# A recurrent mixer and a routed expert layer: finished expert rows scattered from each pair into the output

## The chip, the cores and the metric
The kernel runs on one core of a Trainium2 chip. The metric is the device time of one execution in microseconds; the median of three runs of the kernel before is 650.63 us (649.58 to 650.96).

## What is computed
Input x is (4, 1024, 128), float32. A first layer normalises x, makes queries, keys, values, gates and decays, and runs a recurrence over time with an 8x8 state for each of 16 heads. Its output is laid out so that only every third token gets a non-zero value:

```python
z = jnp.zeros_like(o)
out3 = jnp.stack([z, z, o], axis=2).reshape(B, 3 * N, H, HD)
out = out3[:, -N:]
```

So only a third of the tokens (342 of 1024 in each sequence, the *mixed* rows) is changed by the first layer; the *other* rows keep their x. The second layer adds to every row a shared network and one of 16 experts:

```python
logits = x @ w_router.T
_, top_idx = jax.lax.top_k(logits, TOP_K)            # TOP_K = 1
scores = jax.nn.sigmoid(logits) * mask
masked_inputs = scores.T[:, :, None] * x[None, :, :]
gate_up = jnp.einsum('eth,ehf->etf', masked_inputs, gate_up_proj)
expert_out = jnp.einsum('etf,efh->eth', up * jax.nn.silu(gate), down_proj)
out = shared + expert_out.sum(axis=0)                # then x + out
```

## The kernel before
**Rows.** `xf` holds the residual, 33 rows of 128 numbers in each of the 128 partitions. Every third one is a mixed row (11, set `MIXED`), the rest are other rows (22, set `OTHERS`). Some of the slots stand for no token.

**The recurrence.** The time axis is cut into chunks, 32 for each sequence. First the matrices and sums of all chunks grow side by side (up to about 308 us). Then `ch_s`, the state at the start of each chunk, is found by a chain of 63 steps on VectorE (DVE), L1569 and L1574: `ch_m` (8x8 matrix of a chunk) times the state gives products `ch_pr`, laid out as [value, output i, input j], with the chunk's own sum as a ninth j that GpSimd (POOL) copies in at L1138; the reduction over j is the next state:

```python
V.tensor_tensor(ch_pr[:, m % 2, :, :, 0:HD], ch_m[r][:, :, i, :]..., ch_s[:, :, i, :]..., ALU.mult)
V.tensor_reduce(ch_s[:, :, i + 1, :].rearrange("p i v -> p v i"), ch_pr[:, m % 2], AX.X, ALU.add)
```

A second recursion of 11 steps (L1461 to L1482, L1982) runs behind it from the states found.

**Experts.** For each set of rows the router's choice gives every row a slot in a list that is sorted by expert and cut into tiles of 128 slots (38 tiles for the other rows, 26 for the mixed ones). Rows times score are scattered by POOL into DRAM (`xs_...`, `scatter_tile`, L1021, one indirect DMA for each of the set's row slots). Tiles are worked on in pairs, `over_pairs`: SP loads the rows of a pair (L515), PE transposes them (`x_transposes`, L1919), multiplies by the two experts' first matrices (`gate_up`, L1925), ScalarE (ACT) takes silu (L900), DVE multiplies (`gate`, L1360), PE transposes (L1932) and multiplies by the second matrices (`down`, L1942) into one PSUM region `b_y`; ACT copies it to `e_y` (`copy_y`, L909), which frees `b_y` for the next pair's `down`, and SP writes it to DRAM (`ys_...`, L522). `RUNS[0]`, 12 pairs of other rows, stands beside the chain, `RUNS[1]`, 7 pairs, beside the second recursion, and `RUNS[2]`, the 13 pairs of the mixed rows, at the end. `over_pairs` writes the last three or four pairs out and puts those before into a loop of two pairs a turn. PE, ACT and DVE work one pair ahead and the loads up to three.

**Shared network.** `shared` works in groups of four row slots (L1855 to L1865 on PE, L859 on ACT, L1346 and L1351 on DVE). `shared_add` adds the result to `xf` and counts `s_fa`. For the other rows it runs beside the first part of the chain, for the mixed ones right ahead of `RUNS[2]`.

**The end.** When the pairs of the other rows are written, POOL gathers them back in row order into SBUF (`gather`, L1037, 22 indirect DMAs from 512.7 us on). DVE adds them to `xf` at L1636, in one instruction of 2,816 elements a partition, ahead of the pairs of `RUNS[2]`. After the thirteenth pair is written, POOL gathers the mixed rows (11 indirect DMAs), DVE adds them in two parts (L1647), and SP and ACT store the sums. SP's stores of the other rows (20, L672 to L676) are in its queue behind the last pair's.

Order is by hand: each engine has its own list, and semaphores count what is ready (`s_et` transposed pairs, `s_eo` finished `e_y`, `s_ey` finished `down`, `s_ew` pairs written, `s_gat` gathered, `s_fin` final rows).

Of the kernel before, what the change touches and what calls it, by code (L numbers as in the profile page):

```python
# [65 lines left out]

def constants():
# [13 lines left out]
    for t in (OTHERS, MIXED):  # L81
        v = valid[:, t.rows]
        parts["valid_" + t.name] = v
        spare = np.where(v, 0, t.tiles * P + np.cumsum(~v.ravel()).reshape(v.shape) - 1)
        parts["spare_" + t.name] = spare
        assert (~v).sum() <= P
    parts["prefer"] = np.tile(E - np.arange(E)[None, :], (P, 1))
# [104 lines left out]
def build(nc, a, out, xs, ys, scr):  # L192

    ctx = ExitStack()
    with ctx:
# [7 lines left out]
        normed = nc.dram_tensor("normed", (B, N, D), F32).ap()  # L203

# [4 lines left out]
        eps = sb("eps", [P, 1])  # L209
        warm = sb("warm", [P, 4])  # L210
# [20 lines left out]
        ch_pr = early[:, at:at + 2 * 4 * HD * (HD + 1)].rearrange("p (b v i j) -> p b v i j", b=2, v=4, i=HD)  # L231
# [87 lines left out]
        for t in (MIXED, OTHERS):  # L319
# [12 lines left out]
            else:  # L332
                rows, scaled = take(t.n * D), take(t.n * D)
                q["rows"] = q["shared"] = [rows[:, j * D:(j + 1) * D] for j in range(t.n)]
                q["scaled"] = [scaled[:, j * D:(j + 1) * D] for j in range(t.n)]
                q["back"] = rows
# [23 lines left out]
        def xT_shared(t, g):  # L360
# [9 lines left out]
        assert 4 * U * P <= left.shape[1]  # L370
        e_in, e_xT = (left[:, k * 2 * U * P:(k + 1) * 2 * U * P].rearrange("p (b u d) -> p b u d", b=2, u=U)
                      for k in (0, 1))
# [40 lines left out]
        s_gat, s_fin, s_out = {t: two("s_gathered_" + t) for t in fb}, sem("s_final"), sem("s_out")  # L413
        s_ends = sem("s_out_ends")
# [3 lines left out]
        PARTS = ((0, MIXED.n // 2 + 1), (MIXED.n // 2 + 1, MIXED.n))  # L418
# [55 lines left out]
        def over_pairs(engine, run, pair):  # L474
# [3 lines left out]
            looped = (n - 3) // 2 * 2  # L478
            with engine.Fori(0, looped // 2) as half:
                i = half * 2  # L480
                for k in (0, 1):
                    pair(i, k, 3)
# [17 lines left out]

        def middle_rows(b):

            n = 3 * SKIP
            return out[b, ROWS - n:(C - 1) * ROWS - n:3, :].rearrange("(g r) d -> g r d", r=L2)
# [25 lines left out]
        def _(sp):  # L530
# [72 lines left out]
            for t in SETS:  # L603
                sp.dma_start(xs[t.name].rearrange("(m p) d -> p m d", p=P),
                             zeros[:, 0:D].unsqueeze(1).to_broadcast([P, t.tiles + 1, D])).then_inc(s_xz, 16)
                sp.dma_start(ys[t.name][t.tiles * P:, :], zeros[:, 0:D]).then_inc(s_xz, 16)
# [59 lines left out]
            pairs_in_out(sp, RUNS[2])  # L666
            n = 3 * SKIP
            last = N - ((C - 1) * ROWS - n)
            sp.wait_ge(s_fin, 1)
            for b in range(B):  # L670
                g0 = b * C
                sp.dma_start(out[b:b + 1, 1:ROWS - n, :], xf[g0:g0 + 1, n + 1:, :]).then_inc(s_out, 16)  # L672
                for q in (1, 2):
                    sp.dma_start(out[b, ROWS - n + q:(C - 1) * ROWS - n:3, :].rearrange("(g r) d -> g r d", r=L2),
                                 xf[g0 + 1:g0 + C - 1, q::3, :]).then_inc(s_out, 16)
                    sp.dma_start(out[b:b + 1, N - last + q:N:3, :],  # L676
                                 xf[g0 + C - 1:g0 + C, q:last:3, :]).then_inc(s_out, 16)
            for part, (lo, hi) in enumerate(PARTS):
                sp.wait_ge(s_fin, 2 + part)
                for b in range(B):  # L680
                    sp.dma_start(middle_rows(b)[:, lo:hi, :], xf[b * C + 1:b * C + C - 1, 3 * lo:3 * hi - 2:3, :]
                                 ).then_inc(s_out, 16)
            sp.wait_ge(s_out, 16 * 7 * B)
            sp.wait_ge(s_ends, 16 * 2 * B)
# [1405 lines left out]
```

## Time and profile before

| | |
|---|---|
| median of the runs | 650.63 us (649.58 to 650.96, 3 runs) |
| the profiled execution | 648.87 us, span of its instructions 647.1 us |
| mean granted TensorE clock | 0.946 of 2.4 GHz |
| busy, share of the span | PE 80%, DVE 76%, POOL 56%, ACT 40% |
| chain that ended last, by engine | PE 35%, DVE 29%, issue 14%, POOL 12%, DMA 4%, ACT 3% |
| DMA | 41.79 MB in 46,946 packets |

The time of an execution is a little longer than its span. The span begins with the first instruction and ends with the last; a time in the time line is counted from its start. PEld is the load of a matrix into PE, which overlaps the products. Busy shares are averages over stages with different limits, so the time line of a stage says more than they do.

### The profile page before, as it was taken

The page shows a single profiled execution, that of the slowest core. Times are in us where ns is not written, and L with a number is a line of the kernel's source. Part 1 is how long each engine was busy: PE and PEld are TensorE (multiplying, and loading weights), DVE is VectorE, ACT ScalarE, POOL GpSimd, SP SyncE. Part 2 cuts the span into 40 slices and gives each one's busy share as a digit, 9 for nine tenths or more (in the row PEclk, how much of TensorE's full clock was granted, in tenths as well). Part 3 has the DMA queues.
Part 4 walks back from the last instruction along what each step waited for, and adds up shares of the span by engine and source line. Part 5 has one row for each costly group of instructions (what it writes and reads, how often), then busy time and mean ns, then how long its engine had stood idle before and what let it go on. Part 6 is the DMA issues. An engine that isn't in the chain of part 4 may idle for free.

```text
span 647.1 us, 7400 instructions
## 1 busy us (share of the span) xinstructions
PE 516.5 (80%) x1809; PEld 269.2 (42%) x1810; DVE 489.2 (76%) x787; ACT 257.0 (40%) x542; POOL 363.1 (56%) x353
## 2 busy tenths in 40 slices
PE   3889899999999885777776889789999956398830
PEld 2543434444444332322444455434443353355520
DVE  5697999989898998999799997788999656322201
ACT  4477543444444432112442345524554115044510
POOL 2378776757576564764786343567766574600033
PEclk9999999999999999988999899989999968889985
DMA  7701138400000691000711133101100011112134
GB/s 179 191 18 32 33 89 217 113 1 1 1 1 1 171 344 38 1 0 0 187 43 41 42 97 73 50 9 32 32 16 9 13 54 32 53 50 65 57 85 114
DMA packets 46946, 41.79 MB, mean 65 GB/s; under 512 B 4700, under 2 KB 40360, under 8 KB 46536
## 3 DMA queue, kind: packets, MB, share of 16 engines
q1 hardware_dynamic: 43332, 35.61, 20.2%
q0 software_dynamic: 2448, 5.38, 3.0%
q10 hardware_dynamic: 1136, 0.46, 0.3%
q8 instruction: 12, 0.20, 0.1%
q14 instruction: 18, 0.15, 0.1%
HBM read 23.80 MB, written 17.63 MB: 64 GB/s over the span
## 4 chain that ended last, share of the span: by engine, by line
PE 35%; DVE 29%; issue 14%; POOL 12%; DMA 4%; ACT 3%; SPq 0%; POOLq 0%; DVEq 0%; ACTq 0%
PE ps L1925 10%; DVE grown L1468 9%; PE ps L1942 5%; POOL grown L1091 4%; DVE ps L1502 4%; PE ps L1878 3%; PE ps L1932 2%; DVE early L1569 2%; DVE grown L1490 2%; PE ps L1982 2%; PE ps L1683 2%; POOL uv L1008 2%; PE ps L1879 2%; POOL early L1037 2%; PE ps L1983 2%
## 5 line engine op out<-in xcount | busy, mean ns | idle before, releaser
L1091 POOL TENSOR_TENSOR grown<-grown 128x512 f32<-128x512 f32 x64 | 80.5, 1267 | 91.6 <-DVE grown L1490 91.6
L1468 DVE TENSOR_TENSOR grown<-ps,steps 128x1536 f32<-128x1536 f32 x64 | 112.1, 1752 | 1.6
L1878 PE MATMUL ps<-grown,cst 128*128 128x512 f32 x128 | 72.7, 650 | 25.3 <-DVE grown L1468 24.7
L883 ACT ACTIVATE uv<-ps 128x512 f32<-128x512 f32 x64 | 38.1, 597 | 104.8 <-DVE grown L1490 104.8
L1925 PE MATMUL ps<-steps 128*128 x128 | 68.8, 635 | 8.4 <-issue 8.2
L1008 POOL TENSOR_TENSOR uv<-uv,steps 128x512 f32<-128x512 f32 x64 | 67.4, 1075 | 1.9 <-ACT uv L883 1.9
L1879 PE MATMUL ps<-grown,cst 128*128 128x512 f32 x128 | 67.1, 606 | 0.0
L1360 DVE TENSOR_TENSOR e_h<-rk,ps 128x256 f32<-128x256 f32 x64 | 25.4, 418 | 53.4 <-ACT rk L900 34.6
L1888 PE MATMUL ps<-uv,cst 128*128 128x512 f32 x128 | 60.4, 594 | 0.6 <-POOL uv L1008 0.6
L1167 POOL TENSOR_TENSOR early<-state,qT 128x512 f32 x22 | 37.1, 1688 | 34.0 <-DVE state L1482 34.0
L1490 DVE TENSOR_TENSOR grown<-ps,steps 128x512 f32<-128x512 f32 x64 | 43.3, 676 | 7.4 <-PE ps L1878 7.4
L1502 DVE TENSOR_TENSOR ps<-ps,grown 128x512 f32<-128x512 f32 x60 | 41.6, 693 | 9.4 <-POOL grown L1091 9.4
L1037 POOL DMA_INDIRECT early<-ys_mixed,slots_mixed x11 | 10.5, 956 | 64.7 <-DMA ys_mixed<-e_y 61.7
L1496 DVE TENSOR_TENSOR ps<-ps,steps 128x512 f32<-128x512 f32 x64 | 44.1, 689 | 1.1 <-PE ps L1879 1.0
L1878 PEld LDWEIGHTS ps<-grown,cst 128*128 128x128 f32 x128 | 21.0, 196 | 57.2 <-DVE grown L1468 51.2
L1138 POOL COPY early<-early 128x32 f32<-128x32 f32 x63 | 27.2, 434 | 28.1 <-DVE early L1574 28.0
L1569 DVE TENSOR_TENSOR early<-early 128x256 f32<-128x256 f32 x63 | 40.1, 636 | 1.3
L900 ACT ACTIVATE rk<-ps 128x256 f32<-128x256 f32 x64 | 23.9, 383 | 39.9 <-PE ps L1925 38.2
L1879 PEld LDWEIGHTS ps<-grown,cst 128*128 128x128 f32 x128 | 25.2, 197 | 32.2 <-issue 32.2
L1942 PE MATMUL ps<-steps,e_hT 128*128 x256 | 35.9, 284 | 2.8 <-ACT e_hT L904 2.7
L1888 PEld LDWEIGHTS ps<-uv,cst 128*128 128x128 f32 x128 | 24.2, 190 | 31.8 <-issue 29.6
L1942 PEld LDWEIGHTS ps<-steps,e_hT 128*128 128x128 f32 x256 | 31.5, 191 | 9.1 <-issue 8.0
(228 smaller groups left out, 1008.0 us busy)
## 6 DMA issues: line engine op xcount, KB each, us to landing
steps<-gate_up_proj SPq DMA_DIRECT2D x1, 4096.0 KB, 16.7
xs_others<-zeros SPq DMA_DIRECT2D x1, 2496.0 KB, 11.0
steps<-xs_others SPq DMA_DIRECT2D x19, 128.0 KB, 2.2
ys_others<-e_y SPq DMA_DIRECT2D x19, 128.0 KB, 1.8
early<-chain_m SPq DMA_DIRECT2D x4, 512.0 KB, 6.3
xf<-x SPq DMA_DIRECT2D x4, 495.0 KB
normed<-early SPq DMA_DIRECT2D x28, 64.0 KB, 1.7
xs_mixed<-zeros SPq DMA_DIRECT2D x1, 1728.0 KB, 8.9
```

The lines of the kernel that those rows point to most:

```text
L1008: return G.tensor_tensor(wide(dst, w), wide(src, w), per_col(tile, k, 1, h, w), ALU.mult)
L1091: G.tensor_tensor(decayed[:, h], decayed[:, h], work[:, h, 1], ALU.add).then_inc(s_add[h], 1)
L1468: V.tensor_tensor(grown[:, :, h].rearrange("p e (x w) -> p e x w", w=HD), st, per_col(tile, FF, 3, h, HD), ALU.mult).then_inc(s_prod[h], 1)
L1490: V.tensor_tensor(wide(work[:, h, 1], HD), wide(ps[h][:, 1], HD), per_col(tile_of(i), PP, 1, h, HD), ALU.mult).then_inc(s_uterm[h], 1)
L1496: V.tensor_tensor(wide(bank[2 * h], HD), wide(bank[2 * h], HD), per_col(tile_of(i), K, 1, h, HD), ALU.mult).then_inc(s_term[h], 1)
L1502: V.tensor_tensor(dst, bank[2 * h], decayed[:, h], ALU.add).then_inc(s_state[h], 1)
L1569: V.tensor_tensor(ch_pr[:, m % 2, :, :, 0:HD], ch_m[r][:, :, i, :].rearrange("p j i -> p i j").unsqueeze(1) .to_broadcast([P, 4, HD, HD]), ...
L1878: T.matmul(bank[2 * h + 1], c["block"], work[:, h, 1], start=True, stop=True).then_inc(s_usum[h], 1)
L1879: T.matmul(bank[2 * h], c["minus"], work[:, h, 0], start=True, stop=True).then_inc(s_red[h], 1)
L1888: T.matmul(bank[4 + h], c["ident"], vterm[:, h], start=i in (0, L1), stop=i + 1 in (L1, NT)).then_inc(s_ba[h], 1)
L1925: T.matmul(b_gu(run, b)[u], e_xT[:, b, u], gu[:, bass.ds(ex * (2 * F), 2 * F)], start=True, stop=True).then_inc(s_eg, 1)
L1942: ins = T.matmul(b_y(run)[:, u * D:(u + 1) * D], e_hT[:, u, f * P:(f + 1) * P], dw[:, bass.ds(ex[u] * F + f * D, D)], start=(f == 0), stop ...
```

## The change
Four things are changed.

1. **Mixed rows go straight from the pair into the output.** Each scattered mixed row carries a 129th number, its token's row in the output (`token_mixed`, `q["sent"]`, DRAM tensor `slot_rows`); slots without a row hold 4096, one past the last row. SP loads rows of 129 numbers (`load_rows`). POOL turns the pair's two columns of row numbers into integers (`tokens`). `add_base` on DVE takes the place of ACT's `copy_y`: PSUM plus the pair's *base* rows gives `e_y`. Then two indirect DMAs for each pair write `e_y` to the output rows; numbers above 4095 are dropped by a bounds test.
2. **Base rows.** The residual with the shared network's part (`xf`, mixed rows) is scattered by slot into `ys_mixed` ahead of the pairs, 11 indirect DMAs, with the row numbers of pairs 0 and 1 taken between them; `load_base` brings a pair's 256 rows back. `ys_mixed` is zeroed as a whole at the start, and `slot_rows` filled with rows of zeros and 4096.
3. **Other rows.** Their add is cut in two (12 and 10 row slots) and stands behind `add_base` of pairs 0 and 1. SP stores them two DMAs a pair between its loads, after waiting for both halves (`s_fin` 2). The gathers, adds and stores of the mixed rows at the end are gone, and pairs 0 and 1 of this run are written out ahead of the loop.
4. **The chain.** `ch_pr` is laid out as [value, input j, output i], so that the product reads and writes runs of eight; the reduction steps over eight elements.

```diff
-        ch_pr = early[:, ...].rearrange("p (b v i j) -> p b v i j", b=2, v=4, i=HD)
+        ch_pr = early[:, ...].rearrange("p (b v j i) -> p b v j i", b=2, v=4, i=HD)
...
+            alone = 2 if run.t is MIXED else 0
+            looped = alone + (n - 3 - alone) // 2 * 2
+            for k in range(alone):
+                pair(0, k, n - 1 - k)
...
+            def load_rows(k):
+                sp.wait_ge(s_et, k + run.g0 - 1 if k >= 2 else run.g0)
+                if k >= 2:
+                    sp.wait_ge(s_to, k - 1)
+                sp.dma_start(e_row[:, k % 2], x_in[:, k * U:(k + 1) * U, :]).then_inc(s_ei[k % 2], 16)
+
+            def load_base(k):
+                sp.wait_ge(s_eo, k + run.g0)
+                sp.dma_start(e_base[:, k % 2], base_in[:, k * U:(k + 1) * U, :]).then_inc(s_eb[k % 2], 16)
...
+            for k in range(3):
+                load_rows(k)
+            sp.wait_ge(s_based, 16 * MIXED.n)
+            for k in range(2):
+                load_base(k)
+            for k in range(2, run.n):
+                if k + 1 < run.n:
+                    load_rows(k + 1)
+                load_base(k)
+                if k == 2:
+                    sp.wait_ge(s_fin, 2)
+                for b, part in stores[2 * k - 4:2 * k - 2]:
+                    store_others(b, part)
...
-            pool.wait_ge(s_fa, GA[MIXED.name] + len(MIXED.groups))
-            m = RUNS[2].n
-            gather(MIXED, (RUNS[2].base[0] + (m + 1) // 2, RUNS[2].base[1] + m // 2))
+            for g, (lo, hi) in enumerate(MIXED.groups):
+                pool.wait_ge(s_fa, GA[MIXED.name] + g + 1)
+                for j in range(lo, hi):
+                    G.indirect_dma_start(ys[MIXED.name], ... q["idx"][:, j:j + 1] ..., xf[:, MIXED.rows[j]], None
+                                         ).then_inc(s_based, 16)
+                    if j in TOKENS_AT:
+                        tokens(TOKENS_AT.index(j))
+            for k in range(run.n):
+                if k + 2 < run.n:
+                    tokens(k + 2)
+                pool.wait_ge(s_to, k + 1)
+                pool.wait_ge(s_eo, k + run.g0 + 2)
+                for u in range(U):
+                    G.indirect_dma_start(out_rows, ... e_to[:, k, u:u + 1] ..., e_y[:, k % 2, u], None,
+                                         bounds_check=B * N - 1, oob_is_err=False).then_inc(s_sent[k % 2], 16)
...
-            V.tensor_tensor(rows_of(xf, OTHERS, 0, OTHERS.n), rows_of(xf, OTHERS, 0, OTHERS.n),
-                            tiles_of(fb[OTHERS.name]["back"], OTHERS), ALU.add).then_inc(s_fin, 1)
...
+                add_base(i, k)
+                if ahead > 3 and k < 2:
+                    lo, hi = ((0, 12), (12, OTHERS.n))[k]
+                    dve.wait_ge(s_gat, 16 * OTHERS.n)
+                    V.tensor_tensor(rows_of(xf, OTHERS, lo, hi), ..., ALU.add).then_inc(s_fin, 1)
```

`add_base` waits for the pair's `down`, its base rows and the scatter of `e_y` two pairs before.

POOL, behind the gathers of the other rows: L1021 scatters mixed rows and L1037 gathers before; the list before ends so.

```order
L1037 DMA early<-ys_others,slots_others 128x128 x21
L1021 DMA xs_mixed<-early,slots_mixed 3456x128 [waits s_scaled,s_slots,s_slots_zeroed]
L1021 DMA xs_mixed<-early,slots_mixed 3456x128 [waits s_scaled] x10
L1037 DMA early<-ys_mixed,slots_mixed 128x128 [waits s_e_written1,s_e_written0,s_f_added]
L1037 DMA early<-ys_mixed,slots_mixed 128x128 x10
L195 UNCONDITIONAL_BRANCH
```

The same place in the changed kernel, up to the second pair's scatters (L1060 scatters rows, L1225 base rows, L1220 is `tokens`, L1237 writes to the output):

```order
L1060 DMA slot_rows<-early,slots_mixed 3456x129 [waits s_scaled] x10
L1225 DMA ys_mixed<-xf,slots_mixed 3456x128 [waits s_f_added]
L1225 DMA ys_mixed<-xf,slots_mixed 3456x128 x3
L1225 DMA ys_mixed<-xf,slots_mixed 3456x128 [waits s_f_added]
L1220 CAST e_to<-steps 128x2 [waits s_e_transposed]
L1225 DMA ys_mixed<-xf,slots_mixed 3456x128 x3
L1225 DMA ys_mixed<-xf,slots_mixed 3456x128 [waits s_f_added]
L1220 CAST e_to<-steps 128x2 [waits s_e_transposed]
L1225 DMA ys_mixed<-xf,slots_mixed 3456x128 x2
L1220 CAST e_to<-steps 128x2 [waits s_e_transposed]
L1237 DMA out<-e_y,e_to 4096x128 [waits s_e_out,s_e_tokens]
L1237 DMA out<-e_y,e_to 4096x128
```

The gathers behind the last pair are gone; eleven scatters stand ahead of the first pair's output, and two scatters and a copy follow for each pair.

SP, where the mixed pairs begin in the changed kernel (L691 is `load_rows`, L695 `load_base`, L703 and L705 are stores of the other rows):

```order
L691 DMA steps<-slot_rows 128x2x129 [waits s_e_transposed,s_scattered_mixed]
L691 DMA steps<-slot_rows 128x2x129 [waits s_e_transposed]
L691 DMA steps<-slot_rows 128x2x129 [waits s_e_tokens,s_e_transposed]
L695 DMA uv<-ys_mixed 128x2x128 [waits s_e_out,s_bases_scattered]
L695 DMA uv<-ys_mixed 128x2x128 [waits s_e_out]
L691 DMA steps<-slot_rows 128x2x129 [waits s_e_tokens,s_e_transposed]
L695 DMA uv<-ys_mixed 128x2x128 [waits s_e_out]
L703 DMA out<-xf 1x256 [waits s_final]
L705 DMA out<-xf 330x1x128
L691 DMA steps<-slot_rows 128x2x129 [waits s_e_tokens,s_e_transposed]
```

Before, this was a load ahead of each pair and a store behind it; now the fourth load of rows stands behind the wait for the base rows, and the fifth behind the wait for both halves of the other rows' add and two stores.

DVE, the start of the mixed pairs in the changed kernel (L1423 is `gate`, L1709 `add_base`, L1719 the other rows' add):

```order
L1423 TENSOR_TENSOR e_h<-rk,ps 128x256 [waits s_e_silu]
L1709 TENSOR_TENSOR e_y<-ps,uv 128x256 [waits s_e_written0,s_e_base0,s_e_y]
L1719 TENSOR_TENSOR xf<-xf,early 128x6x256 [waits s_gathered]
L1423 TENSOR_TENSOR e_h<-rk,ps 128x256 [waits s_e_silu,s_e_h_transposed]
L1423 TENSOR_TENSOR e_h<-rk,ps 128x256 [waits s_e_silu]
L1709 TENSOR_TENSOR e_y<-ps,uv 128x256 [waits s_e_written1,s_e_base1,s_e_y]
L1719 TENSOR_TENSOR xf<-xf,early 128x5x256 [waits s_gathered]
```

Before, the list had one add of 128x11x256 ahead of the first `gate`, and nothing but `gate` in the pairs.

## Rows read from the trace of the kernel before

**Rows 1.** Time line, 620 to 638 us: start us, us, engine, line, operation, names, [idle before]
```profile
620.89 0.38 ACT L909 ACTIVATE e_y<-ps 128x256 f32<-128x256 f32 x1 [1.45 <-PE ps L1942]
621.72 0.32 SPq L672 DMA_DIRECT2D out<-xf  x1
622.09 1.02 SPq L674 DMA_DIRECT2D out<-xf  x1
...
623.91 0.99 POOL L1037 DMA_INDIRECT early<-ys_mixed,slots_mixed  x1 [61.66 <-DMA ys_mixed<-e_y]
...
636.52 0.95 POOL L1037 DMA_INDIRECT early<-ys_mixed,slots_mixed  x1 [0.30 <-issue]
```
**Rows 2.** Time line, 557 to 567 us
```profile
557.83 0.97 POOL L1021 DMA_INDIRECT xs_mixed<-early,slots_mixed  x1 [0.30 <-issue]
...
558.32 3.08 DVE L1636 TENSOR_TENSOR xf<-xf,early 128x2816 f32<-128x2816 f32 x1
559.10 3.15 POOL L1021 DMA_INDIRECT xs_mixed<-early,slots_mixed  x1 [0.30 <-issue]
...
565.96 0.66 PE L1919 MATMUL ps<-cst,steps 128*128 128x128 f32 x2 [8.15 <-DMA steps<-xs_mixed]
```
**Rows 3.** Time line, copies of the first three mixed pairs' results
```profile
574.26 0.38 ACT L909 ACTIVATE e_y<-ps 128x256 f32<-128x256 f32 x1 [0.52 <-PE ps L1942]
...
578.05 0.38 ACT L909 ACTIVATE e_y<-ps 128x256 f32<-128x256 f32 x1 [0.61 <-PE ps L1942]
...
582.46 0.38 ACT L909 ACTIVATE e_y<-ps 128x256 f32<-128x256 f32 x1 [0.53 <-PE ps L1942]
```
**Rows 4.** Busy time by stretch: length, PE, PEld, DVE, ACT, POOL busy (x), PEclk, DMA, GB/s
```profile
566.00:572.00 6.00, 5.53 (x15) 2.72 (x16) 0.84 (x2) 1.83 (x5) 0.00 (x0) 0.66 0.15 44
...
580.00:590.00 10.00, 9.06 (x49) 5.91 (x48) 2.27 (x6) 5.53 (x14) 0.00 (x0) 1.00 0.23 66
```
**Rows 5.** Groups by line and shape: count | busy us, mean ns | idle before
```profile
L1569 DVE TENSOR_TENSOR early<-early 128x256 f32<-128x256 f32 x63 | 40.1, 636 | 1.3
L1574 DVE TENSOR_REDUCE early<-early 128x32 f32<-128x288 f32 x63 | 28.6, 455 | 5.1 <-POOL early L1138 3.2
L1360 DVE TENSOR_TENSOR e_h<-rk,ps 128x256 f32<-128x256 f32 x64 | 25.4, 418 | 53.4 <-ACT rk L900 34.6 <-PE ps L1932 18.7
L1138 POOL COPY early<-early 128x32 f32<-128x32 f32 x63 | 27.2, 434 | 28.1 <-DVE early L1574 28.0
...
L1271 DVE TENSOR_TENSOR early<-early 128x352 f32<-128x352 f32 x1 | 0.9, 880 | 0.0
L1326 DVE TENSOR_TENSOR early<-ps,early 128x176 f32<-128x176 f32 x1 | 0.5, 465 | 0.0
L1328 DVE TENSOR_TENSOR early<-early 128x176 f32<-128x176 f32 x1 | 0.3, 342 | 0.0
```
**Rows 6.** Time line: two adds of the shared network, and the second recursion's start
```profile
334.40 0.69 DVE L1351 TENSOR_TENSOR xf<-xf,ps 128x512 f32<-128x512 f32 x1
...
341.65 0.69 DVE L1351 TENSOR_TENSOR xf<-xf,ps 128x512 f32<-128x512 f32 x1
...
401.72 0.90 POOL L1127 DMA_DIRECT2D state<-chain_s  x1 [2.27 <-DMA chain_s<-early]
...
408.17 0.38 ACT L909 ACTIVATE e_y<-ps 128x256 f32<-128x256 f32 x1 [1.45 <-PE ps L1942]
```
**Rows 7.** DMA issues: queue, count, KB each, median us from issue to landing
```profile
steps<-xs_mixed SPq DMA_DIRECT2D x13, 128.0 KB, 2.1
ys_mixed<-e_y SPq DMA_DIRECT2D x13, 128.0 KB, 1.8
...
early<-chain_b SPq DMA_DIRECT2D x4, 256.0 KB, 3.7
...
xs_mixed<-early,slots_mixed POOLq DMA_INDIRECT x11, 2.2
```
**Rows 8.** The page's DMA line: busy tenths in 40 slices
```profile
DMA  7701138400000691000711133101100011112134
```

More of the change, by code:

```diff
@@ L332, in build @@
             else:
-                rows, scaled = take(t.n * D), take(t.n * D)
+                rows, scaled = take(t.n * D), take(t.n * (D + 1))
                 q["rows"] = q["shared"] = [rows[:, j * D:(j + 1) * D] for j in range(t.n)]
-                q["scaled"] = [scaled[:, j * D:(j + 1) * D] for j in range(t.n)]
-                q["back"] = rows
+                q["sent"] = [scaled[:, j * (D + 1):(j + 1) * (D + 1)] for j in range(t.n)]
+                q["scaled"] = [r[:, 0:D] for r in q["sent"]]
+                q["token"] = scaled.rearrange("p (n d) -> p n d", d=D + 1)[:, :, D]
                 q["lg"] = take(t.n * E)
@@ L667, in _, with store_others @@
+            def load_base(k):
+                sp.wait_ge(s_eo, k + run.g0)
+                sp.dma_start(e_base[:, k % 2], base_in[:, k * U:(k + 1) * U, :]).then_inc(s_eb[k % 2], 16)
             n = 3 * SKIP
             last = N - ((C - 1) * ROWS - n)
-            sp.wait_ge(s_fin, 1)
-            for b in range(B):
+            def store_others(b, part):
                 g0 = b * C
[L672 to L684, printed above, removed]
+                if part == 0:
+                    sp.dma_start(out[b:b + 1, 1:ROWS - n, :], xf[g0:g0 + 1, n + 1:, :]).then_inc(s_out, 16)
+                elif part < 3:
+                    sp.dma_start(out[b, ROWS - n + part:(C - 1) * ROWS - n:3, :].rearrange("(g r) d -> g r d", r=L2),
+                                 xf[g0 + 1:g0 + C - 1, part::3, :]).then_inc(s_out, 16)
+                else:
+                    sp.dma_start(out[b:b + 1, N - last + part - 2:N:3, :],
+                                 xf[g0 + C - 1:g0 + C, part - 2:last:3, :]).then_inc(s_out, 16)
@@ new lines, in _ @@
+            stores = [(b, part) for b in range(B) for part in range(5)]
+            for k in range(3):
[11 more added lines that the diff above has]
+                    store_others(b, part)
@@ L685, in _ @@
+            sp.wait_ge(s_out, 16 * 5 * B)
+            for k in (0, 1):
+                sp.wait_ge(s_sent[k], 16 * U * ((run.n + 1 - k) // 2))
         @block.scalar
@@ L996, in _ @@
             pairs(RUNS[2])
-            n = 3 * SKIP
-            last = N - ((C - 1) * ROWS - n)
-            act.wait_ge(s_fin, 3)
-            for b in range(B):
-                g0 = b * C
-                act.dma_start(out[b:b + 1, 0:1, :], xf[g0:g0 + 1, n:n + 1, :]).then_inc(s_ends, 16)
-                act.dma_start(out[b:b + 1, N - last:N:3, :], xf[g0 + C - 1:g0 + C, 0:last:3, :]).then_inc(s_ends, 16)
         def pool_tt(dst, src, tile, k, h, w):
```

102 lines of the change are left out of this document (69 added, 33 removed).

## The prediction
> **What bounds the kernel now.** I read the end first, in the time line: it shows what is left after the last matrix work. The last pair's result is copied out of PSUM at 620.89 to 621.27. POOL then waits until it has landed in DRAM and issues eleven gathers, from 623.91 to 637.47; DVE's add and the stores of the sums follow, and the span ends at 647.1 [rows 1]. So 25.8 us (647.1 - 621.27) hold no matmul: a round trip of the results through DRAM. That is the part the change can remove.
>
> Next the start of the last run of pairs. Indirect transfers follow each other every 1.27 us (557.83, 559.10). The last one took 3.15 us instead of 0.97: it stood beside DVE's 3.08 us add of the other rows, which began at 558.32. Only when it had landed could the first pair be loaded, and its first transposes ran at 565.96 [rows 2]. In the pairs the reader is to look at the ends of the PSUM copies: 574.64, 578.43, 582.84, and 621.27 for the thirteenth. That is 38.4 us for the ten pairs after the third, and 4.4 or 3.8 us each in turn; PE fills them at the full clock (9.1 of 10 us busy) [rows 1, 3, 4].
>
> Last the chain of states, 308 to 398 us. A step is a product of 0.64 us and a reduction of 0.46 us on DVE [rows 5]. Beside it run six groups of the other rows' shared network, 7.25 us apart (334.40, 341.65), then twelve pairs. The recursion behind waits for the last of these pairs' copies, 408.17 + 0.38, while the chain's last result was sent on at 401.72 [rows 6].
>
> **The change part by part**, against the profiled execution (span 647.1, time 648.87; that is 1.76 below the median of the runs, 650.63, so I carry the difference over to the median).
>
> *The end.* Gone: the wait for the written pair, 11 gathers, two adds, the stores of the mixed rows. New behind the last pair: DVE's add (0.42 us, by the 128x256 products from PSUM [rows 5]; it stands for the copy of 0.38) and two scatters. POOL started 0.8 us after what it waited for (landing 1.8 us after the issue at 621.3, so 623.1, to 623.91 [rows 1, 7]); the second issue comes 1.27 later and lands 2.2 us after it began [rows 2, 7]: 4.3 us in place of 25.8. **Minus 21.5.**
>
> *Base rows.* POOL gets 11 more scatters, ahead of the pairs' own. DVE's long add no longer stands beside the last row scatter, so this begins at 559.10 and takes 0.97. The eleventh base scatter begins 11 x 1.27 later, plus two small POOL copies for the row numbers (0.43 us each by the 128x32 copy [rows 5], part of it in the usual gap: 0.6 for both): 559.1 + 14.0 + 0.6 = 573.7; it lands at 575.9. SP loads the first two bases (0.4 us an issue, 2.1 to land): at 578.0 the first is there, and the first add ends at 578.4, not 574.6. **Plus 3.8.** Queued behind this wait on SP is the load of pair 3's rows: 576.7 + 2.1 = 578.8. PE needs them ahead of pair 1's last products, so these run 579.2 to 580.4.
>
> *The other rows' add.* It was 3.08 us in an idle stretch; now 12 and 10 row halves, about 1.75 and 1.48 us by the same rate (0.15 us + 1.04 ns an element), behind the first and second base add. The first holds gate 2, and add 1 ends at 581.4 (was 578.43: plus 3.0). The second ends at 582.9. SP waits for it (s_fin), issues two stores (0.32 and 1.02 [rows 1]), and only then loads pair 4's rows: 584.4 + 2.1 = 586.5. PE stands before their transposes; transposes, products and add take 0.4 + 1.1 + 0.5 + gaps, so add 2 ends at 588.7, not 582.84: **plus 5.9** in all, which contains the 3.8. From pair 3 on SP is ahead again: stores of at most 1.9 us a pair, and a load is issued a pair and a half before PE needs it.
>
> *The clock.* In the 6 us behind PE's long idle stretch the granted clock was 0.66 on average, a mixture of the lower level (1.2 GHz) and the higher (2.4), and from 580 to 590 it was 1.00 [rows 4]. PE now idles about 5 us twice: before pair 1's last products and before pair 2's. The missing 0.34 of 6 us is 2 us of lost work; for the two together I set none to 2.5 us on the path, **plus 1.2**.
>
> *Loop.* Two pairs stand alone ahead of it, so one turn less: the difference of 4.4 and 3.8, **minus 0.5**.
>
> *POOL in the pairs.* Per pair two scatters and a copy: 2 x 1.27 + 0.4 = 2.9 us of 3.9; hidden by PE's work. The bounds test on the row numbers is in no row; I take 0.97 us a scatter as the nearest, with ends 0.97 and 3.15 (the held one). ScalarE loses its copy, off the path. DVE's loop gets a third instruction and register waits; it is idle over half of it.
>
> *Zeroing and 516-byte rows.* SP zeroes 3.5 MB instead of 1.8 for this set. That falls in slices 7 and 8 of 40 (16.2 us each), and behind them stand five slices with no DMA time [rows 8]: hidden. Rows of 129 numbers in place of 128 may load slower; zero to 1.6 us each (the next size, 256 KB, landed in 3.7 [rows 7]), twice on the path. I take zero.
>
> *The chain.* The product now reads and writes runs of eight; the reduction steps over eight elements (32 bytes). Rows: a 128x256 product read in runs takes 0.42, the chain's 0.64. A 128x176 add takes 0.34 with runs and 0.47 with one SBUF operand at a step of 44 bytes (L1328, L1326), 0.70 ns an element; a 128x352 add with a step of 88 bytes 0.88 (L1271), where 0.15 us and 1.04 ns an element make 0.52, so 1.0 ns an element [rows 5]. So the product gains 0.21 us; if the reduction pays the same for its 288 elements it loses 0.20 to 0.29. The sum is 0 to +0.08 a step, 63 steps: 0 to +5. If a single stream pays nothing, a step gains 0.21 us, a group at most 0.35 (then PE and ScalarE lead), six groups 2; the pairs behind do not gain, since they are PE's with or without a chain (4.0 us each in both runs). I take **0**: L1326 is a single SBUF stream too, its other operand being PSUM. The Trainium skill (SBUF — State Buffer, "Door 1: The DMA port swizzle") speaks against this edit in the same way: SBUF is read in lines of 16 bytes, and a step onto a new line each time costs, beyond 4 fp32 elements. By that rule alone the reduction would pay and the sum stay at 0; the trace agrees with it on two-operand instructions, and shows no reduction with a step.
>
> *Sum:* -21.5 + 5.9 + 1.2 - 0.5 + 0 = **-14.9**; 647.1 becomes 632.2, and the median 650.6 becomes **635.7**.
>
> **Rivals.**
> 1. *The reduction's step is free* (25%). For: a reduction reads one stream only. Against: L1326. Another 2 us: 633.7.
> 2. *516-byte rows load slowly* (14%). No row has them. Twice 1.6 on the path, perhaps a little in the loop: 639.
> 3. *POOL takes the pairs over, in part* (7%). At 1.9 us a scatter (double) a pair needs 2 x 2.2 + 0.4 = 4.8 us, 0.9 over PE's 3.9, twelve times: 646.
> 4. *POOL is held* (4%): a scatter to tested row numbers costs as much as the one that was held, 3.15. A pair takes 2 x 3.45 + 0.4 = 7.3, the last add comes at 578.4 + 88 = 666, the end at 673, time 676: slower. It decides from about 2.2 us a scatter: 578.4 + 12 x 5.4 + 4.3 + 1.2 reaches about 648. For it: POOL can be held by DVE, as the row shows. The Trainium skill (SBUF — State Buffer, "SBUF: two separate sides") calls this a lock on a shared port, taken among others by a DVE instruction with two SBUF inputs. By that rule only the two long adds would hold scatters here, for 3.2 us in all, in time that POOL has spare. Against the rival: in the loop DVE reads one PSUM operand each time, and beside such instructions scatters took 0.97 [rows 2].
> 5. *That the change doesn't do what it says*: the gathers are gone from the order of POOL; nothing for it.
>
> **Numbers.** Forecast 50%, rivals 25, 14, 7, 4. Around the forecast the unknown terms are -1.7 (clock 0 and a little) to +2.5 (chain, clock). The range leaves out rival 4, most of 3 and the far end of 1: 631 to 641. A measurement tells 0.2%, 1.3 us, from no change; all cases but the fourth are far above it. Faster 0.95, same 0.01, slower 0.04.
>
> **What would show it.** Right: no row of gathers from ys_mixed; two scatters of about 0.97 us per pair; about 5 us from the last products to the end; adds 0, 1, 2 ending near 578.4, 581.4, 588.7; PE waiting for a load of slot rows before pair 2's transposes; product near 0.42 and reduction near 0.66 us; the recursion's first products near 408.6. Wrong: scatters above 1.5 us, pairs above 4 us with POOL as releaser, or pairs that start before 575.

## The result, and the profile after

The changed kernel takes 642.15 us (median of 4 runs, 641.85 to 642.69) where the kernel before takes 650.41 beside it: a ratio of 0.9875, interval 0.9858 to 0.9892. It is faster, as forecast, but by 8.3 us and not by 14.9; the range of 631 to 641 does not hold it. The profiled execution took 641.85 us, with a span of 639.7 in place of 647.1. The forecast for the span was 632.2.

One thing has to be known to compare single profiles (*before* is that of the kernel before, *after* that of the changed kernel, the others carry the names of the experiments). In the stretch from 512 to 546 us, ahead of the mixed pairs, PE's granted clock was 0.75 of 2.4 GHz in the profiles of before, a1, a3, a4, b1, b3, b4, c1 and c2, and 0.70 in those of after, a2, b2, c3 and c4, a mixture of its two levels (1.2 and 2.4 GHz) each time. With 0.70 the way from the first gather of the other rows to the shared network's first add for the mixed rows is 1.8 us longer (35.93 us in after, 34.14 in a1). From 240 to 300 us the clock also differs, and the chain starts anywhere from 306.7 to 310.2 us. So the first transposes of the mixed pairs stand at 560.6 to 565.7 us in kernels that are the same up to there, and runs of one kernel lie up to 6 us apart (c1: 645.56 to 651.94). So I take distances inside a profile, and medians.

The end in the changed kernel, in the time line (start us, us, engine, line, operation, names, idle before), which answers to [rows 1]:

```profile
627.15 0.42 DVE L1709 TENSOR_TENSOR e_y<-ps,uv 128x256 f32<-128x256 f32 x1 [0.35 <-PE ps L2016]
628.43 0.98 POOL L1237 DMA_INDIRECT out<-e_y,e_to  x1 [1.50 <-DVE e_y L1709]
629.63 0.42 DVE L1709 TENSOR_TENSOR e_y<-ps,uv 128x256 f32<-128x256 f32 x1 [2.06 <-PE ps L2016]
629.71 0.98 POOL L1237 DMA_INDIRECT out<-e_y,e_to  x1 [0.30 <-issue]
631.00 0.98 POOL L1237 DMA_INDIRECT out<-e_y,e_to  x1 [0.30 <-issue]
632.29 0.98 POOL L1237 DMA_INDIRECT out<-e_y,e_to  x1 [0.30 <-issue]
```

The gathers are gone. The last add ends at 630.05 and the last scatter is issued until 633.27. Nothing is busy after that, and yet the span ends at 639.7, which is 9.65 us after the last add. What fills this time is in the view of the block's own line, L202 (queue, instruction, count: shortest, median and longest ns, first and last start):

```profile
L202 POOLq DRAIN  x1: 8258/8258/8258, 631.2 to 631.2; - x1
L202 SPq COMPARE_BRANCH  x1: 38/38/38, 634.5 to 634.5; - x1
L202 SPq DRAIN  x1: 13/13/13, 634.7 to 634.7; - x1
L202 SPq EVENT_SEMAPHORE  x1: 17/17/17, 639.6 to 639.6; - x1
```

SP has seen all transfers land at 634.5. POOL's queue drains from 631.2 to 639.5, which is 6.2 us beyond the end of its last scatter, and the last instructions of the other engines' queues start at 639.6 to 639.7, behind it. The same line in the kernel before, where it was number L195:

```profile
L195 POOLq DRAIN  x1: 14907/14907/14907, 628.4 to 628.4; - x1
L195 SPq COMPARE_BRANCH  x1: 38/38/38, 646.7 to 646.7; - x1
L195 SPq DRAIN  x1: 13/13/13, 646.9 to 646.9; - x1
```

There the drain ended at 628.4 + 14.9 = 643.3, and POOL's last gather had been issued until 637.47: it reached 5.8 us beyond the last gather, nearly as far as in the changed kernel, and was hidden behind the stores.

The start of the mixed pairs, which answers to [rows 2, 3]:

```profile
559.61 0.97 POOL L1060 DMA_INDIRECT slot_rows<-early,slots_mixed  x1 [0.30 <-issue]
...
564.32 0.66 PE L1993 MATMUL ps<-cst,steps 128*128 128x128 f32 x2 [5.96 <-DMA steps<-slot_rows]
...
573.71 0.97 POOL L1225 DMA_INDIRECT ys_mixed<-xf,slots_mixed  x1 [0.31 <-issue]
...
575.97 0.87 SPq L695 DMA_DIRECT2D uv<-ys_mixed  x2
576.93 0.42 SPq L691 DMA_DIRECT2D steps<-slot_rows  x1
578.18 0.42 DVE L1709 TENSOR_TENSOR e_y<-ps,uv 128x256 f32<-128x256 f32 x1 [6.19 <-DMA uv<-ys_mixed]
578.52 1.75 DVE L1719 TENSOR_TENSOR xf<-xf,early 128x1536 f32<-128x1536 f32 x1
...
579.50 1.65 POOL L1237 DMA_INDIRECT out<-e_y,e_to  x1 [4.62 <-DVE e_y L1709]
579.86 1.91 PE L2016 MATMUL ps<-steps,e_hT 128*128 x8
...
581.81 0.42 DVE L1709 TENSOR_TENSOR e_y<-ps,uv 128x256 f32<-128x256 f32 x1 [0.88 <-PE ps L2016]
582.15 1.48 DVE L1719 TENSOR_TENSOR xf<-xf,early 128x1280 f32<-128x1280 f32 x1
...
585.10 0.51 SPq L691 DMA_DIRECT2D steps<-slot_rows  x1
...
587.74 0.44 PE L1993 MATMUL ps<-cst,steps 128*128 128x128 f32 x2 [2.09 <-DMA steps<-slot_rows]
...
589.98 0.42 DVE L1709 TENSOR_TENSOR e_y<-ps,uv 128x256 f32<-128x256 f32 x1 [3.38 <-PE ps L2016]
```

This came as drawn: the last row scatter is no longer held, the last base scatter begins at 573.71, DVE waits 6.19 us for base rows, PE waits twice for a load of slot rows, and adds 0, 1 and 2 end at 578.60, 582.23 and 590.40 (forecast 578.4, 581.4, 588.7, with 1.2 us more for the clock).

The chain, by the groups by line and shape (count | busy us, mean ns of one), against [rows 5]:

```profile
L1637 DVE TENSOR_REDUCE early<-early 128x32 f32<-128x288 f32 x63 | 42.6, 676 | 4.3 <-POOL early L1178 2.2
L1632 DVE TENSOR_TENSOR early<-early 128x256 f32<-128x256 f32 x63 | 27.3, 433 | 1.3
L1178 POOL COPY early<-early 128x32 f32<-128x32 f32 x63 | 19.3, 307 | 34.4 <-DVE early L1637 34.2
```

The product fell from 636 to 433 ns, the reduction rose from 455 to 676: together 18 ns more a step. The chain as a whole kept its length, as its first reduction shows, here in before and in after:

```profile
309.86 0.46 DVE L1574 TENSOR_REDUCE early<-early 128x32 f32<-128x288 f32 x1 [0.21 <-POOL early L1138]
308.93 0.68 DVE L1637 TENSOR_REDUCE early<-early 128x32 f32<-128x288 f32 x1 [0.17 <-POOL early L1178]
```

From there until its last result is sent on it took 91.9 us before (to 401.72) and 91.6 after (to 400.48).

### The profile page after: what moved, and what is told of

Same layout as the page of the kernel before. It is cut to its first block, busy times and chain, and to the rows that moved or that the text cites. A ratio compares the mean times of both kernels' runs of the same rounds, so it can differ in the third digit from the quotient of the medians.

```text
span 639.7 us, 7393 instructions
## 1 busy us (share of the span) xinstructions
PE 522.9 (82%) x1809; PEld 273.2 (43%) x1810; DVE 493.5 (77%) x799; ACT 252.4 (39%) x530; POOL 382.3 (60%) x394
## 4 chain that ended last, share of the span: by engine, by line
PE 34%; DVE 31%; issue 16%; POOL 13%; ACT 3%; DMA 2%; SPq 1%; POOLq 0%; DVEq 0%; ACTq 0%
DVE grown L1531 10%; PE ps L1999 8%; PE ps L2016 5%; POOL grown L1131 5%; DVE ps L1565 4%; PE ps L1952 3%; DVE early L1637 3%; PE ps L2006 2%; PE ps L2056 2%; POOL uv L1045 2%; DVE early L1632 2%; DVE grown L1553 2%; PE ps L1757 2%; POOL slot_rows L1060 2%; PE ps L2057 2%
## 5 line engine op out<-in xcount | busy, mean ns | idle before, releaser
L1131 POOL TENSOR_TENSOR grown<-grown 128x512 f32<-128x512 f32 x64 | 80.5, 1268 | 91.7 <-DVE grown L1553 91.7
L1999 PE MATMUL ps<-steps 128*128 x128 | 70.1, 646 | 8.2 <-issue 8.2
L1423 DVE TENSOR_TENSOR e_h<-rk,ps 128x256 f32<-128x256 f32 x64 | 25.2, 417 | 42.7 <-ACT rk L943 29.4
L1637 DVE TENSOR_REDUCE early<-early 128x32 f32<-128x288 f32 x63 | 42.6, 676 | 4.3 <-POOL early L1178 2.2
L1237 POOL DMA_INDIRECT out<-e_y,e_to x26 | 26.2, 1008 | 27.0 <-DVE e_y L1709 22.6
L1178 POOL COPY early<-early 128x32 f32<-128x32 f32 x63 | 19.3, 307 | 34.4 <-DVE early L1637 34.2
L2016 PE MATMUL ps<-steps,e_hT 128*128 x256 | 37.2, 290 | 2.7 <-ACT e_hT L947 2.7
```

The source lines that it names most:

```text
L1131: G.tensor_tensor(decayed[:, h], decayed[:, h], work[:, h, 1], ALU.add).then_inc(s_add[h], 1)
L1999: T.matmul(b_gu(run, b)[u], e_xT[:, b, u], gu[:, bass.ds(ex * (2 * F), 2 * F)], start=True, stop=True).then_inc(s_eg, 1)
L2016: ins = T.matmul(b_y(run)[:, u * D:(u + 1) * D], e_hT[:, u, f * P:(f + 1) * P], dw[:, bass.ds(ex[u] * F + f * D, D)], start=(f == 0), stop ...
```

## The experiments

Two questions: what the 5.3 us are that the end took beyond the forecast (theories A to D in the texts below), and which of the terms at the pairs' start hold. Edits are against the changed kernel where nothing else is said.

**a1: POOL waits for its scatters to land.**

```diff
+            for k in (0, 1):
+                pool.wait_ge(s_sent[k], 16 * U * ((run.n + 1 - k) // 2))
```

> The changed kernel (time 642.15, span 639.7; last scatters issued 631.00 and 632.29, landed about 634.6), and POOL itself waits for both counts of landed scatters before its list ends. Theory A: POOL's drain ends a fixed 6 us after its last indirect DMA was issued, whatever POOL does meanwhile: span 639.7 unchanged, time 642 +- 1. Theory B: the drain is some 6 us of work that begins only when POOL's list has ended: POOL then ends at about 634.8 + 6 = 641, time 643.5 or more. Theory C: the drain only waits for the landed bytes, so behind a wait for them it is over at once: span about 635.5, time 638.

641.82 us (639.28 to 643.32), ratio 0.9881 [0.9857, 0.9905]. The median tells nothing: it lies at theory A's value, and two of the four runs took 643.2 and 643.3 us, as theory B has it, the two others 639.3 and 640.4. The drain's rows do:

```profile
L202 POOLq COMPARE_BRANCH  x1: 38/38/38, 630.9 to 630.9; - x1
L202 POOLq DRAIN  x1: 6197/6197/6197, 631.1 to 631.1; - x1
```

With everything landed at 630.9 the drain still took 6.2 us. The end came 7.8 us behind the last scatter's issue (628.74 + 0.98 = 629.72, to 637.5), where after has 6.4 (633.27 to 639.7). So the drain is not a wait for bytes: it takes 6.2 us that begin when POOL's list has ended. Theory B.

**a2: no scatters for the last pair.**

```diff
-            for k in range(run.n):
+            for k in range(run.n - 1):
```

> The changed kernel without the two scatters of the thirteenth pair (the output lacks these 256 slots' rows); SP waits for the last add instead. POOL's last indirect DMA is then that of the twelfth pair, issued about 627.6 + 1.3 + 1 = 629.9 at the end, the last add ends at 630.05. Theory A (a fixed 6.2 us behind the last indirect DMA): span about 636.1, time 638.5. Theory C (the end follows the landing of the last bytes, about 2.4 us behind the issue): span about 632.5, time 635. If the drain is tied to neither but to the end of the other engines' lists, it stays near 639.

639.85 us (639.18 to 639.99), 0.984 [0.9823, 0.9856]: 2.3 us less. POOL's last issue ended at 631.74 and the span at 638.0, 6.3 later; SP was done at 633.2. The end moves with POOL's list, not with the landing. (Counted with the router of the reference and its inputs, the mixed rows fill 17 of the 26 tiles. So the last four pairs hold no token's row and their scatters write nothing; with these inputs a2 leaves nothing out of the output, unlike what the text above says. POOL's issues for them take 0.98 us all the same.)

**a3: the rows' loads first.**

```diff
-            for k in range(3):
+            for k in range(4):
                 load_rows(k)
             sp.wait_ge(s_based, 16 * MIXED.n)
...
-                if k + 1 < run.n:
+                if 3 < k + 1 < run.n:
                     load_rows(k + 1)
                 load_base(k)
-                if k == 2:
+                if k == 3:
                     sp.wait_ge(s_fin, 2)
-                for b, part in stores[2 * k - 4:2 * k - 2]:
+                for b, part in stores[2 * k - 6:2 * k - 4] if k > 2 else []:
```

> The changed kernel with two loads moved in SP's list: pair 3's rows ahead of the wait for the base rows, pair 4's rows ahead of the wait for the other rows' add, whose stores begin a pair later. Theory 1 (the two waits of PE for a load of slot rows, 4.4 and 2.1 us, set pairs 1 and 2): add 1 is then held by the base rows and DVE's long adds only, add 2 ends about 4 us earlier (586.4 instead of 590.4), and the time is 638 (637 to 639.5). Theory 2 (the base rows and the long adds on DVE set them, loads only fill the gap): add 2 ends less than 1.5 us earlier, time 640.7 to 642.

636.91 us, 0.9802 [0.9788, 0.9816]: 5.2 us less. From the first transposes to the end of add 2 it takes 21.9 us (560.89 to 582.80) where after has 26.1 (564.32 to 590.40): 4.2 us, theory 1.

```profile
574.56 0.42 DVE L1709 TENSOR_TENSOR e_y<-ps,uv 128x256 f32<-128x256 f32 x1 [4.88 <-DMA uv<-ys_mixed]
...
577.23 0.42 DVE L1709 TENSOR_TENSOR e_y<-ps,uv 128x256 f32<-128x256 f32 x1
...
582.38 0.42 DVE L1709 TENSOR_TENSOR e_y<-ps,uv 128x256 f32<-128x256 f32 x1 [0.40 <-PE ps L2016]
```

Add 2 follows add 1 in 5.2 us instead of 8.2: that is pair 4's load, which stood behind the wait for DVE's second long add and two stores. Add 1 follows add 0 in 2.7 instead of 3.6, but it does so in b1 too (2.66), where no load was moved and pair 1's last products took 1.23 us and not 1.91. So moving pair 3's load is not shown to have gained anything at add 1; against b1 3.1 of 3.8 us are pair 2's (8.3 to 5.2), the rest lies ahead of add 0.

**a4 and c1: the chain alone.** a4 undoes part 4 of the change in the changed kernel; c1 makes it in the kernel before:

```diff
-        ch_pr = early[:, ...].rearrange("p (b v i j) -> p b v i j", b=2, v=4, i=HD)
+        ch_pr = early[:, ...].rearrange("p (b v j i) -> p b v j i", b=2, v=4, i=HD)
```

> The changed kernel with the chain's product laid out as before (product 636 ns, reduction 455 ns, POOL's copy 434 ns in place of 433, 676 and 307). By the sum of the groups (-18 ns a step for the old one, 63 steps) the old layout would be 1.1 us faster if the chain were the bound; the time line showed the opposite, the new one 1.3 us ahead at the start of the second recursion, through POOL's shorter copy, and given back behind it. Theory 1 (a step's price is the same in both): 642.1 +- 1, no difference to be told. Theory 2 (the shorter copy counts, and what was lost behind has another cause): 643.4. Theory 3 (only DVE's sum counts): 641.0.

> The kernel before with part 4 of the change alone (chain's product in runs, reduction with a step). Theory 1 (a step of the chain has the same price, 1.11 us of DVE against 1.09): 650.3 +- 1, no difference. Theory 2 (POOL's shorter copy, 307 ns for 434, counts): 1.2 us less, 649.1. Theory 3 (the reduction's 18 ns count): 1.1 us more.

a4: 640.8 us (638.41 to 642.79), 0.986 [0.9834, 0.9885], which overlaps that of after. c1: 649.28 us, 0.9995 [0.9976, 1.0014]. The groups follow the layout in both (product and reduction 638 and 455 ns in a4, 436 and 677 in c1). a4 leans to theory 3 and c1 to theory 2, opposite ways and within the spread. The profiles settle more than the times: from the first reduction to the last result sent on it takes 91.7 to 91.9 us with the old layout (before, b3, b4, a4) and 91.5 to 92.1 with the new one. The chain's new layout is worth nothing that can be measured, either way.

**b1, b2, b3: the block's end without POOL's drain.**

```diff
-        block = ctx.enter_context(nc.Block())
+        block = ctx.enter_context(nc.Block(no_gpsimd_drain=True))
```

b1 is the changed kernel with this line, b2 adds the edit of a3, b3 is the kernel before with it. SP's waits for the last landings stay.

> The changed kernel, its instructions the same; only the block's end is built without the drain of POOL's queue (SP still waits until every transfer has landed). Theory B (6.2 us of POOL's own drain, which starts when POOL's list ends, set the end): the end follows SP's wait for the last landing, about 2.4 us behind the last issue, instead of 7.2 us: span 4 to 5 us shorter, time 637.5 (636.5 to 638.5). Theory D (some 6 us belong to the end of any such program, whichever engine they are booked on): 642 +- 1.

> The same block end together with the loads moved ahead in SP's list (the kernel of a3_rows_first, 636.9). Theory B: the two gains add, 636.9 - 4.6 = 632.3 (631 to 633.5). Theory D: 636.9 +- 1.

> The kernel before, its block's end built without POOL's drain. There the drain ended at 643.3, the landing of the last stores at about 646.7: it was hidden, with 3.4 us to spare. Theory B: 650.4 +- 1, no difference. Theory D: no difference either.

b1: 636.1 us, 0.9788 [0.9762, 0.9815], 6.0 us less than after. In its profile no DRAIN stands on POOL's queue, and the end is SP's:

```profile
L202 SPq COMPARE_BRANCH  x1: 37/37/37, 630.5 to 630.5; - x1
L202 SPq DRAIN  x1: 13/13/13, 630.7 to 630.7; - x1
```

The last add ends at 626.05 and the span at 631.0: 4.95 us, where after has 9.65. So the drain's own part is 4.7 us; the rest of the 6.0 is not explained by it (b1's profile has the clock of 0.75 in 512 to 546, and after's has 0.70). b2: 632.25 us, 0.9718 [0.9686, 0.9749]: the two gains add. b3: 649.23 us, 0.9987 [0.9971, 1.0004]: in the kernel before the drain cost nothing.

**b4: the kernel before without its last adds and stores** (SP waits for the gathers instead; the mixed rows are missing from the output).

> The kernel before without the last adds and stores of the mixed rows (the output lacks these rows' expert part and the rows themselves); SP waits for the gathers' landing, which were issued until 637.5 and land at about 639.5. Theory B: with DVE, ACT and SP out of the way POOL's drain sets the end, 637.5 + 5.8 = 643.3 and 0.2: span 643.5, time 646.2 by the median, 4 us less than before. Rival C (the end follows the landing): span 640, time 642.5.

645.84 us, 0.9919 [0.9893, 0.9945]: 4.5 us less, not the 8 that the landing would give.

```profile
L195 POOLq DRAIN  x1: 14905/14905/14905, 628.1 to 628.1; - x1
L195 SPq DRAIN  x1: 13/13/13, 639.6 to 639.6; - x1
```

SP had finished at 639.6; the drain ended at 643.0, the span at 643.3. The hidden wait of the kernel before comes out as soon as its cover is gone, which is what the change did.

**c2: the other rows' adds back ahead of the pairs.**

```diff
+            for lo, hi in ((0, 12), (12, OTHERS.n)):
+                dve.wait_ge(s_gat, 16 * OTHERS.n)
+                V.tensor_tensor(rows_of(xf, OTHERS, lo, hi), ..., ALU.add).then_inc(s_fin, 1)
             gate(RUNS[2], 0, 0, 0)
...
                 add_base(i, k)
-                if ahead > 3 and k < 2:
...
```

> The changed kernel with the other rows' two adds moved back ahead of the pairs (behind the shared network's last add, about 559 to 562), the loads as in the change. Theory 1 (the add behind the base adds, and SP's wait for it, put 2 to 3 us on pairs 1 and 2; ahead of the pairs it holds one base scatter for about 2 us): add 2 ends some 2 us earlier, time 640 (639 to 641). Theory 2 (what the held scatter costs and what the pairs gain are equal): 642. Theory 3 (a scatter held ahead of the pairs costs more than the pairs gain): 643 or more.

637.3 us, 0.9822 [0.98, 0.9844]: 4.9 us less, more than theory 1 said. By distance, first transposes to the end of add 2: 22.8 us (561.43 to 584.21) against 26.1, 3.3 us less. Add 1 ends 3.6 us after add 0, as in after; add 2 follows in 4.8 instead of 8.2. So all of it is at pair 2, whose load no longer waits behind DVE's add in the pairs. What the adds hold ahead of the pairs is small:

```profile
555.96 1.83 POOL L1060 DMA_INDIRECT slot_rows<-early,slots_mixed  x1 [0.30 <-issue]
558.10 1.10 POOL L1225 DMA_INDIRECT ys_mixed<-xf,slots_mixed  x1 [0.30 <-issue]
```

That is 0.86 + 0.13 us. The first of them stands ahead of the first transposes; counted from the start of the shared network's last add, which takes it in, it is 29.5 us (554.73 to 584.21) against 32.0 (558.39 to 590.40), 2.5 us less. Moving the add into the pairs was worth nothing as SP's list stood: it saved 1 us of held scatters and put some 3.3 on pair 2. The rest of the 4.9 us between the medians is not explained.

**c3: no base scatters** (the loads stay and read zeros; the output lacks the residual and the shared network's part of the mixed rows).

> The changed kernel without the eleven scatters of the base rows and the wait for them; the loads of base rows stay and read the zeroed tensor (the output lacks the residual and the shared network's part of the mixed rows). It prices the base rows' way, for which the prediction took 3.8 us at pair 0 (5.9 with the other rows' add at pair 2). Theory 1 (base scatters set pair 0, and through the load behind them pair 1 and 2): add 0 ends at about 573, the end comes 5.5 to 6.5 us earlier: 636. Theory 2 (the long adds and the load behind s_fin set pair 2 anyway): 2 us or less earlier: 640.

635.04 us, 0.9781 [0.9761, 0.9802]: 7.1 us less. The last row scatter stands at 559.61 as in after, so here times compare directly:

```profile
572.29 0.42 DVE L1702 TENSOR_TENSOR e_y<-ps,uv 128x256 f32<-128x256 f32 x1 [0.34 <-PE ps L2009]
...
584.50 0.42 DVE L1702 TENSOR_TENSOR e_y<-ps,uv 128x256 f32<-128x256 f32 x1 [4.56 <-PE ps L2009]
```

Add 0 ends 5.9 us earlier, add 2 5.5, the last add 6.0 (624.01). Theory 1: the way of the base rows is dear at pair 0 and never given back. Add 2 still comes 8.5 us after add 1, so the load behind the wait for DVE's long add is a price of its own, paid with or without base scatters. (The medians are 7.1 us apart, 1 more than the last adds; that is not explained.)

**c4: row, token number and base row in one scatter.** The kernel of b2, with rows of 257 numbers: DVE's add of the shared network writes into the tile that POOL scatters, each scatter waits for its group's add, and base rows are loaded from the same DRAM tensor.

```diff
-                V.tensor_tensor(rows_of(xf, t, lo, hi), rows_of(xf, t, lo, hi), ...
+                V.tensor_tensor(fb[t.name]["base"][:, lo:hi, :] if t is MIXED else rows_of(xf, t, lo, hi),
+                                rows_of(xf, t, lo, hi), ...
...
                 for j in range(lo, hi):
-                    G.indirect_dma_start(ys[MIXED.name], ..., xf[:, MIXED.rows[j]], None).then_inc(s_based, 16)
+                    scatter_tile(MIXED, j)
```

> A new version: the kernel of b2_no_drain_rows_first (632.25), in which DVE writes xf plus the shared network's result next to the scaled row and its token number, and POOL scatters the three together, 257 numbers, after the shared network's group: 11 scatters in place of 22. The last one is then tied to the last group's add: it starts about 2 us later than the last row scatter did, and 12 us earlier than the last base scatter did. Theory 1 (with the base rows in time, pairs 0 to 2 follow from the first transposes as before, 16.9 us up to the third result): add 2 ends 2 to 3 us earlier, 629.8 (628.5 to 631.5). Theory 2 (the long adds on DVE set pairs 1 and 2, or rows of 1,028 bytes scatter slowly): 632 or more.

630.31 us (629.44 to 631.95), 0.9713 [0.9693, 0.9733]; b2 had 632.25.

```profile
561.32 0.97 POOL L1059 DMA_INDIRECT slot_rows<-early,slots_mixed  x1 [0.31 <-issue]
...
566.32 0.66 PE L1992 MATMUL ps<-cst,steps 128*128 128x128 f32 x2 [8.41 <-DMA steps<-slot_rows]
...
574.81 0.42 DVE L1708 TENSOR_TENSOR e_y<-ps,uv 128x256 f32<-128x256 f32 x1 [0.34 <-PE ps L2015]
...
583.01 0.42 DVE L1708 TENSOR_TENSOR e_y<-ps,uv 128x256 f32<-128x256 f32 x1 [0.47 <-PE ps L2015]
```

The last scatter begins at 561.32 in place of 573.71, and a scatter of twice the bytes takes the same 0.97 us. First transposes to add 2: 17.1 us, where the kernel before took 16.9. The first transposes now wait for the shared network's last add too; from the start of this add to the end of add 2 it takes 25.5 us (557.95 to 583.43), where before took 25.0, b2 27.2 and after 32.0. So 0.5 us of the change's start is left. c4 has the lowest median of the study, 20 us below the kernel before and 12 below the change. Its 1.9 us on b2 fit the 1.7 of the profiles (27.2 and 25.5), but the ratios to the kernel before, 0.9713 and 0.9718, do not tell the two apart.

## Why the prediction was wrong in size

**The end: the step that failed.** "4.3 us in place of 25.8. Minus 21.5." It counted to the landing of the last scatter and took the span to end there; what POOL's queue does behind its last instruction stood in the sum at nothing, without a reason. The end took 9.65 us: 4.7 of the 5.3 too many are POOL's drain (b1). The other 0.65 b1 still has (4.95): 0.15 ahead of the first scatter and 0.5 from the landing, which SP had seen at 630.5, to the last instruction at 631.0. The drain was in the trace of before, 14.9 us long and hidden, as a queue instruction that no busy share counts. I asked what was late next behind the gathers and did not look at what POOL itself did behind them. The change took away the 3.4 us of cover that the drain had there (643.3 to 646.7), and b4 shows the same limit in the old kernel.

**Base rows: right, in part by luck.** Last scatter at 573.7, first base add at 578.4: measured 573.71 and 578.60. That the scatter is met to 0.01 us is chance: the last row scatter began 0.51 us later than taken (559.61 for 559.10), and the two small copies cost 0.13 and not 0.6. c3 prices the way at 5.9 us against a kernel that has the faster row scatter but no base rows; the forecast's 3.8 was against the kernel before, where the held scatter stood.

**The other rows' add and SP's list: right in kind, 0.5 short with the clock.** Add 2 was forecast for 588.7 + 1.2 = 589.9 and came at 590.40. PE stood idle 4.37 and 2.09 us there, not about 5 twice, and the clock cost about what was put down for it: after the wait of 4.37 us pair 1's last products took 1.91 us where 1.12 is the full-speed time, and pair 2's took 1.67, together 1.3 us for 1.2; from 579 to 586 the granted clock was 0.56. The rest is pair 4's load: its transposes ran 2.64 us after its issue (585.10 to 587.74), where the sum had 2.1. a3 and c2 show that the load behind the second long add was the price of this order: 4.2 us by a3, 2.5 by c2, held scatters deducted.

**Loop: wrong.** No saving, and a loss: from add 2 to add 12 it took 39.65 us, where 38.4 - 0.5 = 37.9 was forecast. That no saving came is a reading of the rows gone wrong. In the kernel before, the copies of pairs 3 and 4 are these:

```profile
586.24 0.38 ACT L909 ACTIVATE e_y<-ps 128x256 f32<-128x256 f32 x1 [0.61 <-PE ps L1942]
...
590.61 0.38 ACT L909 ACTIVATE e_y<-ps 128x256 f32<-128x256 f32 x1 [0.53 <-PE ps L1942]
```

Pairs are counted from 0. With [rows 3] the copies of pairs 2 and 4 come 4.4 us behind the one before them, that of pair 3 comes 3.8 behind, and so it goes on to pair 8. The turn that was taken out of the loop thus had its long step ahead of pair 2's result, and the ten steps behind that kept all of their long ones. Beyond that a turn of two pairs takes 8.28 us and not 8.15, and the waits of PE put down to issue ahead of `gate_up` rose by a little (4.0 us for 8 pairs, before 3.4). The distance also differs from profile to profile: 38.4 us in before, b3 and b4, but 38.84 (a3) to 40.37 (a2) in the changed kernel and its variants. So 0.4 us of loss is in all of them, and more in some; what makes it was not tried and stays open. 1.75 us of the miss are here.

**Chain: right.** The reduction over a step of 32 bytes took 221 ns more for 288 elements, 0.77 ns an element, inside the 0.7 to 1.0 that were worked out from three other instructions; the product gained 203. The Trainium skill (SBUF — State Buffer, "Door 1: The DMA port swizzle") has the cost of a step onto a new 16-byte line, and the trace now agrees for a reduction too. Rival 1 is out. In the profile the shared network's groups ran 1.35 us earlier (325.88 for the second in place of 327.23). The text of a4 puts this down to POOL's shorter copy, but 0.93 of it was there at the chain's first reduction (308.93 in place of 309.86), and the chain is no shorter. From 512 to 547 us it was lost again at a granted clock of 0.70.

**POOL in the pairs: right.** All but one of the 26 output scatters took about 0.98 us, the bounds test cost nothing that shows beside the 0.97 of the others, and a pair was PE's. Rivals 3 and 4 are out. One scatter, at 579.50, took 1.65 us beside DVE's long add of 1.75, and a small copy 1.27 in place of 0.19 beside the second. The Trainium skill's lock (same page, "SBUF: two separate sides") lets a DVE instruction with two SBUF inputs hold a GpSimd instruction that reads SBUF; the trace agrees for the copy. For the issue of a DMA beside such an add the page (there, "Who interferes with whom") infers the opposite, that it is not held; here it was (1.65 us, and 3.15 in the kernel before), and the measurement decides.

**Rows of 516 bytes: right.** They landed in 2.3 us at the median, the 512-byte rows of before in 2.1; rival 2, with its 1.6 us twice, is out. The two loads on the path were taken up 2.45 and 2.64 us after their issue, so 0.4 and 0.5 us more than the 2.1 taken.

Sum of the miss: the end 5.35, add 2 0.5, ten pairs 1.75, together 7.6 us; the span was 639.7 where 632.2 was forecast. By the median it is only 6.5 us (642.15 for 635.7), and that is luck: the forecast carried over the 1.76 us by which the profiled execution of before lay below its median, and that of the changed kernel lay only 0.3 below.

## What to carry to other kernels

When the work at the end of a kernel is cut away, look at every engine's last instruction, also those on its queue that count as no work: in these kernels, whose POOL lists all end with indirect DMAs, the drain that follows took 5.8 to 6.2 us, whether or not the transfers had landed, and what of it nothing else covers is paid (4.7 us here). What a drain takes behind another kind of list, no run shows. Before two loads and a wait are put into one queue, ask who needs the load behind the wait; here two loads moved ahead were worth 4 us, 3 of them by the load that stood behind the wait for DVE's add. And where two scatters by the same row numbers follow each other, one of twice the width cost the same issue here, 0.97 us.

## What the runs showed of the hardware

- POOL's drain at the block's end took 6.2 us behind the end of its list in the changed kernel (8.26 us from 631.2, of which 2.07 lie before the last issue's end; 6.197 alone in a1; 6.1 in a2) and 5.8 in the kernel before and in b4. What it does in this time, and why it is 0.4 us shorter there, is open.
- A scatter of 128 rows of 257 numbers holds POOL for 0.97 us like one of 128 numbers, and lands in 2.4 us against 2.2.
- POOL's copy of 128x32 elements took 307 ns into runs of eight where it had taken 434 with a step.
- PE's granted clock ahead of the mixed pairs was 0.70 or 0.75 for the same work, and with 0.70 this stretch was 1.8 us longer (35.93 against 34.14 us).
- Beside a DVE add with two operands in SBUF, POOL's issue of a scatter took 1.65 us in place of 0.98 (after, add of 1.75 us) and 3.15 in place of 0.97 (before, add of 3.08 us).
